# A two-layer decoder with six blocks on one core: feature transposes in a bank of their own, one-piece causal maxima, and three moved pieces of work

## The reference

```python
def softmax_kernel(data, proj, is_query):
    data_n = data * d ** (-0.25)
    dd = jnp.einsum('bhnd,md->bhnm', data_n, proj)
    diag = 0.5 * jnp.sum(data_n * data_n, axis=-1, keepdims=True)
    stab = jnp.max(dd, axis=-1, keepdims=True) if is_query else jnp.max(dd)
    return ratio * (jnp.exp(dd - diag - stab) + KERNEL_EPS)
...
context = jnp.einsum('bhnm,bhnd->bhmd', kf, v)
out = jnp.einsum('bhnm,bhmd,bhn->bhnd', qf, context, d_inv)
...
x = x + L0_attn(layernorm(x))                       # random features
x = x + L0_xattn(layernorm(x), ctx_1024, ctx_1024, mask)
x = x + L0_ffn(layernorm(x))                        # four trees of depth 8, nodes with biases
x = x + L1_attn(layernorm(x))                       # causal softmax
x = x + L1_xattn(layernorm(x), ctx_1024)
x = x + L1_ffn(x)                                   # top-16 experts of 1024
```

## Time and profile before

| what | value |
|---|---|
| median of 3 runs | 883.47 us (880.09 to 885.48) |
| the profiled execution's own time | 881.07 us |
| its span, first to last instruction | 879.0 us |
| TensorE busy (matmuls) | 698.6 us, 79% |
| VectorE busy | 640.7 us, 73% |
| ScalarE busy | 441.7 us, 50% |
| GpSimd busy | 280.4 us, 32% |
| mean granted TensorE clock, share of full speed | 0.882 |

### The profile page before, as it was taken

One profiled execution on the slowest core, in us unless ns is written; L12 is line 12 of the kernel. 1 busy time (PEld: TensorE's weight loads), 2 busy tenths in 40 slices (PEclk: granted clock), 3 DMA queues, 4 the chain that ended last, 5 costly groups with the idle time before them and its releaser, 6 DMA issues. The chain is left out here.

```text
span 879.0 us, 15168 instructions
## 1 busy us (share of the span) xinstructions
PE 698.6 (79%) x5016; PEld 532.8 (61%) x5016; DVE 640.7 (73%) x2791; ACT 441.7 (50%) x1051; POOL 280.4 (32%) x253
## 2 busy tenths in 40 slices
PE   3776977787848989888687479999876958888898
PEld 1446534444347777676486257655566948877788
DVE  5765557553389697986695457877449999999984
ACT  1213004465058787898664145565732556555562
POOL 3113722201333222331131022121013037777783
PEclk9986557998568999999978689999987979999999
DMA  8600052300389888897555334332000000000000
GB/s 255 143 1 2 4 72 30 45 8 1 126 325 356 346 307 324 308 396 287 199 199 155 99 42 54 53 45 40 2 1 1 1 1 2 4 4 7 4 4 7
DMA packets 42678, 93.67 MB, mean 107 GB/s; under 512 B 4050, under 2 KB 30194, under 8 KB 34408
## 3 DMA queue, kind: packets, MB, share of 16 engines
q0 software_dynamic: 9216, 69.47, 20.7%
q1 hardware_dynamic: 33384, 23.23, 13.4%
HBM read 74.42 MB, written 0.52 MB: 85 GB/s over the span
## 5 line engine op out<-in xcount | busy, mean ns | idle before, releaser
L763 ACT ACTIVATE arena<-arena,hact 128x128 f32<-128x128 f32 x512 | 155.8, 391 | 1.0
L573 POOL TENSOR_TENSOR arena<-arena 128x1024 f32<-128x1024 f32 x64 | 121.3, 1915 | 82.6 <-DVE arena L1233 65.2
L663 ACT ACTIVATE arena<-psum 128x512 f32<-128x512 f32 (+1 forms) x192 | 101.2, 562 | 61.6 <-PE psum L1383 60.8
L1084 DVE CUSTOM_DVE_ANT_0 arena<-arena,fx 128x128 f32<-128x128 f32 x384 | 106.0, 349 | 0.3
L1706 PE MATMUL psum<-arena 128*128 128x128 f32 x688 | 88.5, 287 | 21.3 <-DVE arena L1233 19.3
L894 DVE TENSOR_REDUCE rowmax<-psum 128x2 f32<-128x512 f32 x128 | 81.5, 687 | 29.3 <-PE psum L1365 27.1
L1706 PEld LDWEIGHTS psum<-arena 128*128 128x128 f32 x688 | 84.1, 201 | 24.5 <-DVE arena L1233 12.5
L1595 PE MATMUL psum<-identf,arena 128*128 128x128 f32 x544 | 76.0, 295 | 23.6 <-ACT arena L763 23.1
L1365 PE MATMUL psum<-arena 128*128 128x256 bf16 (+1 forms) x384 | 76.6, 293 | 18.5 <-DVE rowmax L894 10.1
L1595 PE MATMUL psum<-arena,identf 128*128 128x128 f32 x544 | 78.7, 299 | 15.6 <-ACT arena L763 14.2
L816 ACT ACTIVATE psum<-arena,tneg 128x1024 f32<-128x1024 f32 x64 | 71.2, 1114 | 39.6 <-POOL arena L573 14.0
(11 more groups left out here) (220 smaller groups left out, 1222.0 us busy)
## 6 DMA issues: line engine op xcount, KB each, us to landing
arena<-parts SPq DMA_DIRECT2D x144, 64.0 KB
arena<-zeros SPq DMA_DIRECT2D x6, 1232.0 KB
w_sb<-attn_w SPq DMA_DIRECT2D x1, 768.0 KB, 8.1
x<-x_in SPq DMA_DIRECT2D x1, 512.0 KB, 4.3
fx<-ctx_in SPq DMA_DIRECT2D x1, 512.0 KB, 5.2
picked<-mask_in SPq DMA_DIRECT2D x1, 512.0 KB, 6.5
wq_sb<-peer_wq SPq DMA_DIRECT2D x1, 512.0 KB, 7.7
down_sb<-table_down SPq DMA_DIRECT2D x1, 512.0 KB, 8.7
```

The lines of the kernel that those rows point to most:

```text
L573: nc.gpsimd.tensor_tensor(grid[k % 3].rearrange("p (i j) -> p i j", i=PK), sim[:, t, h, :].unsqueeze(2).to_broadcast([P, PK, PK]), sim[:, ...
L663: nc.scalar.activation(probs[k % (2 * HG)][:, 0:w], bank(2 + k % 2, 0, w), ACT.Exp, scale=float(D) ** -0.5).then_inc(probs_ready, 1)
L763: a = nc.scalar.activation(w, w, ACT.Copy, scale=hact[i % 2][:, l:l + 1])
L1084: i = nc.vector.tensor_tensor_reduce(w, w, src, 1.0, r[:, LW * E + l:LW * E + l + 1], ALU.mult, ALU.add, hid[g % 4][:, l:l + 1])
```

## The change

Six edits. The feature transposes go to bank 6, one half (a sub-block of 128 rows) at a time, and ScalarE instead of VectorE copies each half out, adding 1e-4; q's products of the next batch then wait for VectorE's reading of banks 0 and 1 alone (`zq_ready`), and products and half norms have semaphores of their own. The first two key exponentials come before ScalarE's copies of the context. GpSimd splits the node biases behind the first run's work instead of ahead of it. An area's ones come ahead of its parts, and in both runs the third area is filled only behind the first batch's maxima. The causal maxima of a head are one reduction over three blocks of 128, and a `tensor_tensor` joins the last two.

```diff
+                i = nc.vector.tensor_reduce(rowmax[n % 2][:, :, h], bank(k % 2, 0, 3 * P).rearrange("p (s n) -> p s n", n=P),
+                                            AX.X, ALU.max)
-                nc.vector.tensor_reduce(rowmax[n % 2][:, 0, h:h + 1], bank(k % 2, 0, P), AX.X, ALU.max)
-                i = nc.vector.tensor_reduce(rowmax[n % 2][:, 1, h:h + 1], bank(k % 2, P, P + S), AX.X, ALU.max)
...
             def max_parts(n):
...
+            if stage(n) == 2:
+                link(nc.vector.tensor_tensor(rowmax[n % 2][:, 1, :], rowmax[n % 2][:, 1, :], rowmax[n % 2][:, 2, :], ALU.max))
...
 # SP
+            def fixed(i, afresh):
+                if afresh:
+                    pad(i)
+                sp.dma_start(stk[i][KS:KM, :, 1, :], ones...).then_inc(pad_ready[i], 16)
             def run(first, last):
...
+                fixed(first % 3, afresh)
                 place(first)
-                for i in range(3):
-                    if first > B and i == 1:
-                        sp.wait_ge(fh_ready, len(ORDER))
-                    if first > B and i > 0:
-                        pad((first + i) % 3)
-                    sp.dma_start(stk[(first + i) % 3][KS:KM, :, 1, :], ones...)
+                if afresh:
+                    sp.wait_ge(fh_ready, len(ORDER))
+                fixed((first + 1) % 3, afresh)
                 place(first + 1)
                 place_max(first)
+                fixed((first + 2) % 3, afresh)
...
 # GpSimd: the block that splits nbias_sb moves from ahead of power(B) to behind run(*RUNS[0])
...
 # ScalarE
                 act.wait_ge(zq_ready, n + 1)
                 if n >= 1:
-                    act.wait_ge(qft_ps, n)
+                    act.wait_ge(qft_ps, SUB * n)
                 nc.scalar.activation(eq, zq, ACT.Exp).then_inc(eq_ready, 1)
+                for s in range(SUB):
+                    act.wait_ge(qft_ps, SUB * n + s + 1)
+                    nc.scalar.activation(qf_t[:, SUB * n + s, :, :], bank(6).rearrange("p (g n) -> p g n", g=HG),
+                                         ACT.Copy, bias=1e-4).then_inc(qft_ready, 1)
...
 # VectorE, feature batch n
-                dve.wait_ge(dd_ps, n + 1)
+                dve.wait_ge(ddq_ps, n + 1)
...
                 link(nc.vector.tensor_reduce(sv, ddq, AX.X, ALU.max))
+                dve.wait_ge(hn_ps, n + 1)
...
+                dve.wait_ge(dd_ps, n + 1)
                 nc.vector.tensor_reduce(kmax[:, SUB * n:SUB * n + SUB], ...)
...
-                dve.wait_ge(qft_ps, n + 1)
-                nc.vector.tensor_scalar(qf_t[...], psum[:, 0:2 * BANK]..., 1e-4, None, ALU.add).then_inc(qft_ready, 1)
...
 # TensorE
+            features(0, 0)
+            half_norms(0)
+            features(0, 1)
+            for n in range(B):
+                if n + 1 < B:
+                    pre(n + 1)
+                    features(n + 1, 0)
+                turn_q(n, 0)
+                if n + 1 < B:
+                    half_norms(n + 1)
+                    features(n + 1, 1)
+                turn_q(n, 1)
```

More of the change, by code:

```diff
@@ L99, in decoder_program @@
         vaug = [sb(f"vaug{i}", [P, SUB, H, VW]) for i in range(4)]
-        rowmax = [sb(f"rowmax{i}", [P, SUB, H]) for i in range(2)]
+        rowmax = [sb(f"rowmax{i}", [P, 3, H]) for i in range(2)]
         negmax = sb("negmax", [P, SUB, H])
@@ L423, in place_max @@
                 sp.dma_start(stk[n % 3][KS:KM, :, 0, :], mt[n % 2][:, :]).then_inc(max_in[n % 3], 16)
+            def fixed(i, afresh):
+                if afresh:
+                    pad(i)
+                sp.dma_start(stk[i][KS:KM, :, 1, :],
+                             ones[:, :].unsqueeze(1).to_broadcast([KM - KS, H, S])).then_inc(pad_ready[i], 16)
             def run(first, last):
-                if first == B:
+                afresh = first > B
+                if afresh:
+                    sp.wait_ge(leaf_done, len(ORDER) - 2)
+                else:
                     sp.wait_ge(consts, 1)
@@ L578, in _ @@
             pool.wait_ge(kmax_all, 1)
+            power(B)
+            power(B + 1)
+            split(B)
+            split(B + 1)
+            power(B + 2)
+            run(*RUNS[0])
             pool.wait_ge(in_tab, 32)
@@ L589, in _ @@
             nc.gpsimd.tensor_copy(nbias_w[:, 0:1], p[:, 0:1]).then_inc(nbias_ready, 1)
[L590 to L595, removed]
             ffn()
@@ L672, in _ @@
                 if n >= 1:
-                    act.wait_ge(qft_ps, n)
+                    act.wait_ge(qft_ps, SUB * n)
                 nc.scalar.activation(eq, zq, ACT.Exp).then_inc(eq_ready, 1)
-            for half in range(2):
-                act.wait_ge(ctxt_ps, half + 1)
-                copy(ctx_t[:, half * BANK:(half + 1) * BANK], bank(2 + 4 * half), ctxt_ready)
+                for s in range(SUB):
+                    act.wait_ge(qft_ps, SUB * n + s + 1)
+                    nc.scalar.activation(qf_t[:, SUB * n + s, :, :], bank(6).rearrange("p (g n) -> p g n", g=HG),
+                                         ACT.Copy, bias=1e-4).then_inc(qft_ready, 1)
             act.wait_ge(nkmax_ready, 1)
             for n in range(B):
+                if n == 2:
+                    for half in range(2):
+                        act.wait_ge(ctxt_ps, half + 1)
+                        copy(ctx_t[:, half * BANK:(half + 1) * BANK], bank(2 + 4 * half), ctxt_ready)
                 if n >= 2:
@@ L1420, in _, with features, half_norms @@
             pre_v(0)
-            for n in range(B):
+            def features(n, w):
+                if n == 0 and w == 0:
+                    pe.wait_ge(feat_ready, 1)
                 if n >= 1:
[L1423 to L1426, removed]
+                    pe.wait_ge(zk_ready if w else zq_ready, n)
                 pe.wait_ge(qk_ready, n + 1)
                 fw = feat_w[:, :, :].rearrange("p h m -> p (h m)")
-                for w in range(2):
-                    for s in range(SUB):
-                        nc.tensor.matmul(bank(2 * w + s), qk_f[n % 2][:, w, s * P:s * P + P], fw, start=True, stop=True)
+                for s in range(SUB):
+                    i = nc.tensor.matmul(bank(2 * w + s), qk_f[n % 2][:, w, s * P:s * P + P], fw, start=True, stop=True)
+                i.then_inc(dd_ps if w else ddq_ps, 1)
+            def half_norms(n):
                 pe.wait_ge(sq_ready, n + 1)
+                if n >= 1:
+                    pe.wait_ge(zk_ready, n)
                 for w in range(2):
@@ L1436, in _, with turn_q @@
                         i = nc.tensor.matmul(bank(7, j, j + H), sq[:, w, s * P:s * P + P], half16[:, :], start=True, stop=True)
-                i.then_inc(dd_ps, 1)
+                i.then_inc(hn_ps, 1)
+            def turn_q(n, s):
+                pe.wait_ge(eq_ready, n + 1)
+                if n + s >= 1:
+                    pe.wait_ge(qft_ready, SUB * n + s)
+                for g in range(HG):
+                    j = (s * HG + g) * P
+                    i = nc.tensor.transpose(bank(6, g * P, g * P + P), eq[:, j:j + P], identf[:, :])
+                i.then_inc(qft_ps, 1)
+            features(0, 0)
+            half_norms(0)
+            features(0, 1)
+            for n in range(B):
                 if n + 1 < B:
                     pre(n + 1)
[L1440 to L1445, removed]
+                    features(n + 1, 0)
[4 more added lines that the diff above has]
+                turn_q(n, 1)
             def keys_values(n):
@@ L1465, in _ @@
             pe.wait_ge(zk_ready, B)
+            pe.wait_ge(qft_ready, SUB * B)
             for t in range(T):
```

18 lines of the change are left out of this document (6 added, 12 removed).

## The result

The kernel after the change takes 887.5 us (median; 881.1 to 891.8), the kernel before, beside it, 881.72 us (876.3 to 885.5). The ratio is 1.0063, 95% interval 1.004 to 1.0085: slower by 5.8 us, a small change whose interval still leaves out 1, where 16 us were forecast as gained. The profiled execution has a span of 882.7 us against 879.0, at the same mean clock (0.88).

A forecast was written before the change was run, and what follows sets the result against it. No engine is busy throughout; one loop paces the feature batches, TensorE bounds keys and values. Terms -13.7 - 1.4 - 1.5 + 8.1 - 7.0 - 0.3 = -15.8 on 881.07 give 865.3 us, range 854.5 to 874.5.

The forecast's parts named there:

- A: Feature batches: without VectorE's copy and its wait, turns shorten to 11.1 us, the last under 9; -13.7 us.
- B: Start of cross-attention: node biases leave, so VectorE's variance step is not held and TensorE's wait goes; -1.4 us.
- C: First run's start: ones go ahead of parts, so TensorE waits for parts instead, half of 2.97 saved; -1.5 us.
- F: Causal maxima: one reduction of 384 columns replaces each of 64 pairs, mostly beside TensorE's work; -0.3 us.
- D: Behind the first run: GpSimd's node biases hold VectorE's five small operations on batch 6's negated maxima; +8.1 us.
- R2: Rival: stack transfers gain nothing, the rate of parts and not the pads being the limit; 872.3 us, chance 0.10.
- R4: Rival: the feature-batch loop is not shortened, turns stay 13.6 us; 876.5 us, chance 0.06.
- R5: Rival: slower, TensorE at half clock becomes the limit in the feature batches; 884.4 us, chance 0.04.
- R3: Rival: TensorE enters keys and values at full clock, without the earlier gap; 857.3 us, chance 0.07.
- R1: Rival: the late node biases meet nothing, GpSimd yielding or the times missing each other; 857.2 us, chance 0.18.
- E: Second run: third area filled behind the first maxima, so batch 9's parts share queues with one pad; -7.0 us.

The follow-up runs named there:

- e3: Changed kernel with GpSimd's node biases early again, arena still at 384 within 512 bytes: 881.38 us, ratio 1.0016.
- e6: Changed kernel with early node biases, unused bytes placing parts at 0 and arena at 0 within 512 bytes: 863.35 us, ratio 0.9796.
- e7: Changed kernel with early node biases, parts at 384 and arena at 384 within 512 bytes: 881.56 us, ratio 0.9992.
- e8: Changed kernel with early node biases, parts at 384 and arena at 256 within 512 bytes: 861.82 us, ratio 0.9766.
- e10: e4 with SP's old transfer order in the first run alone: 860.28 us, ratio 0.9752.
- e12: Changed kernel, arena at 256, node biases in two pieces: two thirds behind the maximum over partitions, the rest behind split(5): 859.24 us, ratio 0.9742.
- e4: Changed kernel with arena back at 256 and node biases early again: 859.63 us, ratio 0.9756.
- e1: Changed kernel with 384 unused bytes a partition ahead of the arena, putting it back at 256: 864.75 us, ratio 0.9831.
- e13: Changed kernel with early node biases, parts at 256 and arena at 320 within 512 bytes: 876.17 us, ratio 0.9947.
- e14: Changed kernel with early node biases, parts at 256 and arena at 128 within 512 bytes: 883.87 us, ratio 1.0032.
- e5: Changed kernel with early node biases, parts at 256 and arena at 0 within 512 bytes: 861.64 us, ratio 0.9772.

## Why the prediction was wrong, term by term

The sum of the six edits came out near, and a seventh effect was missing. With the arena back in its place the changed kernel takes 864.75 us, where 865.3 was forecast. That closeness is in part luck: A was put 2.6 us too high, B 0.6 and C 1.5, F 3.3 too low, and the loss of D 2.2 too high, and these misses cancel to 0.9.

**The step that failed** is the part "Causal maxima: -0.3 us". It priced the instructions and not the tile that they write into. The wider `rowmax` moves the arena to 384, every copy into a stack writes off its 256-byte block, and that is 22.8 us. None of the rivals had it: R2 came nearest in place (stack transfers as the limit), but took their rate as given. The profile of before showed that such a delay would count: TensorE already waited for parts, 8.99 us ahead of batch 9, 4.41 ahead of batch 6, 4.36 ahead of batch 10, and 0.36 to 0.49 ahead of three later ones.

**A, -13.7:** mechanism right, size less: 11.1 us by the runs, 10.4 by the trace. The first batch gained 2.2 (2.5 forecast), the turns 1.6 and 2.4 (2.5 each), the last turn 3.4 instead of 5.7, the end 0.9 (1.4). The last turn was to last 7.9 us by VectorE's work; it lasts 10.24, since q's maximum starts at 56.08 after an idle 1.28 for the products and the addition waits 0.64 more for the half norms. The granted clock was 0.50, the 1.2 GHz level, from 50 to 55 us in this profile. In e3, whose code is the same up to there, it was 1.00, and the last turn took what VectorE's work asks:

```profile
47.38 1.22 DVE L949 TENSOR_TENSOR arena<-psum,stab 128x1024 f32<-128x1024 f32 x1
...
53.71 1.23 DVE L946 TENSOR_REDUCE stab<-psum 128x32 f32<-128x1024 f32 x1
...
55.20 1.22 DVE L949 TENSOR_TENSOR arena<-psum,stab 128x1024 f32<-128x1024 f32 x1
```

That is 7.8 us with no wait, and e3's key exponentials start at 60.40, where 60.5 was forecast. The thirteen profiles with this code agree: the last turn takes 7.8 us where the clock from 50 to 55 us is 1.00 (e3, e6, e7, e8, e10), 9.0 to 9.2 where it is 0.67 or 0.68 (e12, e4), and 10.2 to 10.5 where it is 0.50 (the other six). So what A had too small in the last turn is its 0.9 us for the low clock. R4 and R5 are out, and R3 too: in after the clock was 0.60 from 60 to 80 us and 0.55 from 80 to 100.

**B, -1.4:** the variance step takes 0.17 us and its wait is gone, as said; worth about 0.8.

**C, -1.5:** nothing. The parts end 0.3 us ahead of the ones, not half of 2.97. "They stood just ahead in the queues" was the evidence for 0, and I took the middle.

**D, +8.1:** right in kind and place, too large. VectorE's negated maxima of batch 6 beside GpSimd's node biases, in after:

```profile
168.26 2.12 POOL L597 TENSOR_TENSOR arena<-arena,nbias_w 3x1020 f32<-3x1020 f32 x1
...
169.01 1.41 DVE L917 TENSOR_SCALAR negmax<-rowmax 128x32 f32<-128x32 f32 x1
...
170.46 0.18 DVE L918 CAST mparts<-negmax 128x32 bf16<-128x32 f32 x1
170.46 1.92 POOL L598 TENSOR_TENSOR nbias_w<-nbias_w,identf 3x1020 bf16<-3x1020 bf16 x1
...
170.67 1.76 DVE L919 TENSOR_TENSOR remax<-negmax,mparts 128x32 f32<-128x32 f32 x1
172.46 2.10 POOL L600 TENSOR_TENSOR bias_p<-bias_p,nbias_w 3x1020 bf16<-3x1020 bf16 x1
172.46 2.13 DVE L920 CAST mparts<-remax 128x32 bf16<-128x32 f32 x1
174.62 1.02 POOL L595 CAST nbias_w<-arena 3x1020 bf16<-3x1020 f32 x1
174.63 1.06 DVE L921 TENSOR_TENSOR mparts<-remax,mparts 128x32 bf16<-128x32 f32 x1
175.72 1.88 POOL L598 TENSOR_TENSOR nbias_w<-nbias_w,identf 3x1020 bf16<-3x1020 bf16 x1
...
175.75 0.41 PE L1422 MATMUL psum<-identb,mparts 128*48 128x128 bf16 x2 [5.24 <-DVE mparts L921]
```

Each held operation ends when GpSimd's does. From the first to the transposes it is 6.7 us instead of 1.4: +5.3. Four of five are held, where the prediction had all five; the second, L918, starts in the same hundredth as GpSimd's L598 and is through in 0.18. By the runs, e1 to e4 gains 5.1 us, and B's 0.8 was given back in it, so D is 5.9 (known to some 4 us; after to e3 gives 6.1 + 0.8). R1 is out.

**E, -7.0:** 7.1 us, mechanism and size right. Batch 9's rows start 13.3 us behind batch 8's, and the wait is 0.91 instead of 8.99.

**F, -0.3:** 3.6 us, apart from the placement. The reduction was estimated right (0.55, measured 0.557), the pair too cheap: "about half" of 0.415 for the smaller one, which takes 0.289, and more of the saving shows in the time than "mostly beside TensorE's work" allowed.

Sum by the runs: -11.1 - 0.8 + 0 + 5.9 - 7.1 - 3.6 = -16.7, and +22.8 for the placement: +6.1, measured +5.8. This agreement is no proof of the terms: they are differences along one chain of runs from before to after, so that they must add up to about the whole.

## What to carry to other kernels

A tile that grows moves every tile declared behind it: list the addresses, modulo 256 bytes, of all tiles that DMAs write in short runs, before and after, and pin or pad them. When a queue takes more time for the same packets and bytes (13.4 to 15.5% here), look at where they land before looking at who competes. And put GpSimd's long operations on SBUF where VectorE reduces from PSUM, not where it makes small SBUF tiles on whose result TensorE waits: each small one lasts till GpSimd's ends, while the row maxima from PSUM kept their 679 to 694 ns in all 128 instances of after, beside the node biases too.

## What was not expected of the hardware

- Runs of 512 bytes written 128 bytes off a multiple of 256 move at 57 GB/s instead of 73, with the DMA engines as busy (0.65 and 0.63). 64 bytes off costs somewhat less (16.5 against 22 us of the whole). The source's place cost nothing (e8, 861.82 us).
- A batch's parts have little slack: some 1.8 us more for each of 12 batches (e13) became 16.5 us of time, some 2 to 2.7 us more became 22.
- The granted clock at the head of the trees differs from profile to profile, whatever the arena's place. The engines there (busy times of the engines, clock, DMA share, GB/s), in after and then in e1:

```profile
216.00:233.00 17.00, 15.96 (x42) 7.95 (x40) 7.24 (x16) 1.15 (x3) 0.38 (x1) 0.50 0.01 1
```

```profile
211.00:225.00 14.00, 12.96 (x46) 7.26 (x45) 7.28 (x17) 1.15 (x3) 0.43 (x1) 0.74 0.00 1
```

  At 0.50, the 1.2 GHz level throughout, GpSimd waits 18.38 us for the leaves' numbers, with the part at 2.4 GHz 14.96. The profiles of before, e4 and e14 are of the first kind, those of e12 and e13 of the second. No kernel was profiled in both ways, but at 50 to 55 us, ahead of all stack copies, e4 has 0.68, e5 0.50 and e6 1.00, and these differ in unused bytes alone; the key exponentials start at 67.60, 65.02 and 60.43 us. So single profiles differ by 3 us at the trees, and by up to 7 at the key exponentials, without a cause that the edit shows, and the prices above are taken from the medians.
- How pads and gathered rows, whose runs are longer, react to the place was not measured apart; in the time of the trees, where the rows are gathered, the place shows no cost (above).
